# A state-space block with a gated mixture of experts: gated products and mixed adapter values kept in place in PSUM

## The reference

```
x = x + tanh(g_xattn) * ssm(ctx, layernorm(x))        # a scan over 512 positions, 16 states
x = x + tanh(g_ffn)   * moe(layernorm(x))

def _fused_linear(x, W, qa, qb, scale, w):
    out = x @ W.T
    a = jnp.einsum('th,krh->tkr', x, qa)
    b = jnp.einsum('tkr,khr->tkh', a, qb)
    mix = jnp.einsum('tkh,tk->th', b, w)
    return out + scale[None, :] * mix
...
def expert(muW, gW, gqa, gqb, gs, uW, uqa, uqb, us, dW, dqa, dqb, ds, w):
    xe = x + w @ muW.T
    gate = jax.nn.silu(_fused_linear(xe, gW, gqa, gqb, gs, w))
    up = _fused_linear(xe, uW, uqa, uqb, us, w)
    return _fused_linear(gate * up, dW, dqa, dqb, ds, w)
```

## Time and profile before

| | |
|---|---|
| median of 3 runs | 1738.85 us (1738.04 to 1742.68) |
| the profiled execution, its own time | 1740.07 us |
| its span, first to last instruction | 1738.3 us |
| PE busy | 1581.6 us, 91% |
| DVE busy | 1171.5 us, 67% |
| POOL, ACT busy | 719.9 us (41%), 621.4 us (36%) |
| PE on the chain that ended last | 63% of the span |
| DVE on that chain | 19% |

### The profile page before, as it was taken

The page is one execution under the profiler, slowest core; times in us unless marked ns, Lnnn a source line. Parts: engine busy times, 40 slices in busy tenths (PEclk is TensorE's granted clock), DMA queues, the critical chain, the costliest instruction groups (busy, mean ns, idle before and its releaser), DMA issues.

```text
span 1738.3 us, 19493 instructions
## 1 busy us (share of the span) xinstructions
PE 1581.6 (91%) x6856; PEld 1162.7 (67%) x6856; DVE 1171.5 (67%) x1629; ACT 621.4 (36%) x973; POOL 719.9 (41%) x524
## 2 busy tenths in 40 slices
PE   4676778888888899999999999999999999999999
PEld 2243456566666667777777777677767787777776
DVE  5786847588898885578888857588888653333333
ACT  5543334444454433433343334443343311111111
POOL 2465513169888850137677601167777100000000
PEclk7798979989999999999999999999999999999999
DMA  3344625878878766558665554756666357456652
GB/s 132 126 165 169 251 81 184 268 264 286 281 260 284 270 239 237 195 201 276 242 223 199 195 189 167 240 211 233 235 238 234 129 199 239 168 192 219 212 189 82
DMA packets 109888, 365.15 MB, mean 210 GB/s; under 512 B 20000, under 2 KB 45600, under 8 KB 94048
## 3 DMA queue, kind: packets, MB, share of 16 engines
q1 hardware_dynamic: 100320, 330.09, 54.3%
q10 hardware_dynamic: 9472, 33.82, 5.7%
HBM read 293.62 MB, written 70.25 MB: 209 GB/s over the span
## 4 chain that ended last, share of the span: by engine, by line
PE 63%; DVE 19%; ACT 7%; issue 6%; DMA 2%; POOL 2%; SPq 0%; ACTq 0%; DVEq 0%; POOLq 0%
PE b_g L653 14%; PE b_u L653 13%; PE b_u L744 7%; DVE ring L1389 4%; PE b_q L744 4%; PE b_q L699 3%; PE b_g L744 3%; DVE ring L1395 3%; PE b_g L717 3%; PE b_g L684 2%; DVE tt L1363 2%; PE b_g L677 2%; ACT b_a L878 1%; PE b_d L636 1%; DVE z L1363 1%
## 5 line engine op out<-in xcount | busy, mean ns | idle before, releaser
L1286 POOL TENSOR_TENSOR ring<-du,rep 128x512 f32<-128x512 f32 x256 | 335.4, 1315 | 199.1 <-DVE du L1464 115.5
L653 PE MATMUL b_g<-xnb,gm 128*128 128x512 f32 (+1 forms) x1440 | 358.2, 398 | 3.0 <-DVE tt L1363 1.5
L653 PE MATMUL b_u<-xnb,gm 128*128 128x512 f32 (+1 forms) x1440 | 349.4, 391 | 1.4 <-DVE xx L1363 1.4
L1389 DVE TENSOR_TENSOR_SCAN ring<-b_a,ring 128x512 f32<-128x512 f32 x256 | 310.6, 1213 | 55.4 <-ACT b_a L878 42.9
L1295 POOL TENSOR_TENSOR yx<-yx,ring 128x512 f32<-128x512 f32 x192 | 262.3, 1366 | 147.7 <-DVE ring L1395 146.5
L653 PEld LDWEIGHTS b_g<-xnb,gm 128*128 128x128 f32 (+1 forms) x1440 | 253.6, 180 | 92.0 <-issue 27.0
L653 PEld LDWEIGHTS b_u<-xnb,gm 128*128 128x128 f32 (+1 forms) x1440 | 257.0, 179 | 73.1 <-DVE xx L1363 2.2
L1363 DVE SCALAR_TENSOR_TENSOR tt<-tt,b_g 128x512 f32<-128x512 f32 (+1 forms) x120 | 81.9, 683 | 208.7 <-ACT tt L878 208.5
L878 ACT ACTIVATE b_a<-delta,a_neg 128x512 f32<-128x512 f32 x256 | 171.8, 679 | 79.1 <-DVE ring L1389 77.0
L744 PE MATMUL b_u<-dwt,hhl 128*128 128x512 f32 (+1 forms) x720 | 186.4, 395 | 0.4 <-DVE hhl L1366 0.4
L878 ACT ACTIVATE tt<-b_g 128x512 f32<-128x512 f32 (+1 forms) x120 | 71.2, 593 | 288.6 <-PE b_u L684 261.0
(11 more groups left out here) (214 smaller groups left out, 2153.2 us busy)
## 6 DMA issues: line engine op xcount, KB each, us to landing
gm<-scr_gm SPq DMA_DIRECT2D x60, 1024.0 KB, 7.8
dwt<-scr_dw SPq DMA_DIRECT2D x30, 1536.0 KB, 6.8
rep<-bc_d ACTq DMA_DIRECT2D x64, 512.0 KB, 5.0
gm<-scr_gm SPq DMA_DIRECT2D x30, 768.0 KB, 4.4
dqt<-scr_dq SPq DMA_DIRECT2D x24, 896.0 KB, 9.6
scr_gm<-gm SPq DMA_DIRECT2D x20, 1024.0 KB, 7.4
scr_dw<-dwt SPq DMA_DIRECT2D x10, 1536.0 KB, 6.2
qat<-scr_qa SPq DMA_DIRECT2D x24, 512.0 KB, 10.6
```

The source lines that it names most:

```text
L653: i = mm(out_b[0:IW[m], :], w, v, start=(n == 0), stop=(n == 11 and not is_routed(s)))
L1286: v.tensor_tensor(ring[:, T % NRING], du[:, T % 4, :], rep[:, N % NREP, 0], ALU.mult).then_inc(pool_dbu, 1)
L1389: v.tensor_tensor_scan(w, ba[T % 2][:], w, 0.0, ALU.mult, ALU.add).then_inc(dve_scan, 1)
```

## The change

Three values move from SBUF into the PSUM bank from which they were computed. h is written over its gate bank `bg[m]` instead of `tt`; `aw` over `b_q`; `dawf` over `b_g0`. ACT rounds from the bank and DVE subtracts from the bank. No instruction is added, removed or reordered on any engine.

Since a bank now holds the value until its low part is made, waits move. Before a later product may write the bank, PE waits for the low part: for chunk 2's gate product and for the next body's first (`up_waits`), for the first `down` product into `b_g1`, for the first `adapter_a` product into `b_g0`, for the `down` product into `b_q`. And ACT's tanh, which writes `tt`, now waits for h where it waited for the low part.

```diff
             def up_waits(s, m):
                 ready(pe, "gm%d" % m, s)
                 if m == 0:
-                    need(pe, dve_h, IC * s)
+                    need(pe, dve_hl, IC * s)
                     if s > 0 and is_routed(s - 1):
-                        pe.wait_ge(dve_dawf, rho(s - 1) + 1)
+                        pe.wait_ge(dve_daw, rho(s - 1) + 1)
                 elif m == 1:
                     need(pe, dve_dn, LC * (s - 1) + 3)
                 else:
-                    pe.wait_ge(dve_h, IC * s + 1)
+                    pe.wait_ge(dve_hl, IC * s + 1)
...
             def adapter_a(s, m):
-                pe.wait_ge(dve_hl, IC * s + m + 1)
                 if m == 0:
                     ready(pe, "dq", s)
-                    pe.wait_ge(dve_h, IC * s + IC)
+                    pe.wait_ge(dve_hl, IC * s + IC)
...
             def down(s, tc, ms=range(IC)):
...
                         ready(pe, "dw", s)
-                        pe.wait_ge(dve_h, IC * s + 2)
+                        pe.wait_ge(dve_hl, IC * s + 2)
...
-                            pe.wait_ge(dve_aw, rho(s) + 2)
+                            pe.wait_ge(dve_awl, rho(s) + 2)
...
             def tanh(s, m):
-                need(act, dve_hl, IC * s + (0, -1, 1)[m])
+                need(act, dve_h, IC * s + (0, -1, 1)[m])
...
-                rounded(hh[0:w, m], tt[0:w, m % 2, :]).then_inc(act_hh, 1)
+                rounded(hh[0:w, m], bg[m][0:w, :]).then_inc(act_hh, 1)
...
-                stt(t, t, 0.5, bu[m][0:w, :], ALU.mult, ALU.mult).then_inc(dve_h, 1)
+                stt(bg[m][0:w, :], t, 0.5, bu[m][0:w, :], ALU.mult, ALU.mult).then_inc(dve_h, 1)
...
-                lo(hl[0:w, m], t, hh[0:w, m]).then_inc(dve_hl, 1)
+                lo(hl[0:w, m], bg[m][0:w, :], hh[0:w, m]).then_inc(dve_hl, 1)
...
-                tt_(aw[:], b_q[:], wr[:, r % 2], ALU.mult).then_inc(dve_aw, 1)
+                tt_(b_q[:], b_q[:], wr[:, r % 2], ALU.mult).then_inc(dve_aw, 1)
...
-                lo(aw_l, aw[:], aw_h).then_inc(dve_awl, 1)
+                lo(aw_l, b_q[:], aw_h).then_inc(dve_awl, 1)
...
-                tt_(dawf[:], b_g0[:], wr[:, r % 2], ALU.mult).then_inc(dve_dawf, 1)
+                tt_(b_g0[:], b_g0[:], wr[:, r % 2], ALU.mult).then_inc(dve_dawf, 1)
...
-                stt(daw_s[:], rnd[:].bitcast(F32), mlo[:], dawf[:], ALU.mult, ALU.add).then_inc(dve_daw, 1)
+                stt(daw_s[:], rnd[:].bitcast(F32), mlo[:], b_g0[:], ALU.mult, ALU.add).then_inc(dve_daw, 1)
```

More of the change, by code:

```diff
@@ L1059, in aw_hi @@
                 act.wait_ge(pe_gu, IC * s)
-                rounded(aw_h, aw[:]).then_inc(act_aw, 1)
+                rounded(aw_h, b_q[:]).then_inc(act_aw, 1)
             def daw_round(s):
                 act.wait_ge(dve_dawf, rho(s) + 1)
-                rounded(rnd[:], dawf[:]).then_inc(act_daw, 1)
+                rounded(rnd[:], b_g0[:]).then_inc(act_daw, 1)
             def shared_0(b, pre_):
```

## The result

The changed kernel takes 1759.95 us (median of 4 runs, 1759.58 to 1760.25), the kernel before 1738.44 beside it; the ratio is 1.0118, 95% interval [1.0101, 1.0136]. That is 21.5 us more, where 14.7 were forecast. The profiled execution took 1759.88 us with a span of 1758.1, so its span is 19.8 longer than that of before. Where they went, by the start of each body's first up product (into `b_u0`) in the two traces: 1.6 us ahead of batch 0's first body, 3.5 in batch 0, 6.0 in batch 1, 7.8 in batch 2, nothing in the first nine bodies of batch 3, 0.9 in the last.

A forecast was written before the change was run, and what follows sets the result against it. PE was taken as the bound from batch 1 on, DVE and PE alternating in batch 0. Batches 1 and 2 (+8.1), last body (+0.7), batch 0 (+2.5) and clock dips (+3.4) give +14.7, 1753.5 us; range 1741 to 1766.

The forecast's parts named there:

- PE as the bound from batch 1 on: Routed bodies from batch 1 on: PE is busy nearly throughout (248.57 of 253 us in batch 2), so its delays add time.
- The six products and the low part: At adapter_a, six products lose 1.36 us of cover; low parts shorten from 1.40 to 0.69: +8.1 us over batches 1 and 2.
- A bank as operand: DVE's low part and h write using PSUM: low part 0.69 us everywhere, h's write bounded by 0.03 either way, taken as 0.
- The clock: Longer PE gaps at adapter_a in experts 0 and 4 bring two new clock dips, +3.4 us, up to +8.5.
- Batch 0: All eight bodies wait at adapter_a, less DVE's gain on low parts and daw_s: +2.5 us, bounds -4 to +9.6.
- rival B: Faster: DVE's chain sets the pace in batches 0 to 2, so its savings shorten bodies; -8.5, 1730 us, chance 0.08.
- The other moved waits are covered: Chunk 2's gate product, the b_q down product and the next body's first product lose nothing, though narrowly.
- The sum: Whole kernel: 8.1 + 0.7 + 2.5 + 3.4 = +14.7 us, forecast 1753.5 us.

The follow-up runs named there:

- experiment 1: Kernel before with only adapter_a's wait moved to chunk 2's low part, every value in SBUF: 1772.39 us, ratio 1.0191.
- experiment 7: Kernel before with h in its gate banks for chunks 0 and 1 only, chunk 2 in SBUF: 1739.11 us; with six down products also moved ahead, 1729.09.
- Experiment 5: Kernel before with h in place in the up product's banks instead of the gate product's, aw and dawf in SBUF: 1728.41 us, ratio 0.9935.
- experiment 4: Changed kernel with adapter_a writing b_u0 and dawf in SBUF: 1734.52 us, ratio 0.9978; with aw also back in SBUF and its old wait: 1729.42, 0.9953.
- experiment 6: Six fourth-chunk down products moved ahead of adapter_a: in the changed kernel 1726.71 us, ratio 0.9935; in the kernel before 1730.78, ratio 0.9958.

## Why the prediction was right, and where its sizes were off

**PE as the bound from batch 1 on** was right: in batches 1 to 3 a body whose nine adapter products had no wait for the low part kept its length to 0.03 us, and a body in which they had one became longer by it, dips aside. PE's idle time in front of these products went from 31.3 us to 47.2 in all, 15.9 more where some 15 were forecast.

**The six products and the low part** were right in sign and nearly in size: 0.67 to 0.69 in experts 2 and 6 where 0.65 stood, 1.37 for 1.3, 0.09 for 0.1. Without dips the batches cost 4.4 and 4.6 us instead of 4.05. Of what is missing in expert 4 and in the last body, 0.2 is one thing: PE starts 0.14 to 0.15 us behind the low part's end, where the row of before had 0.05, and nine products take 2.32 behind a wait and 2.22 without. I had counted the latter in expert 0 only. Expert 4 of batch 2 lost 1.09, 0.4 more than the 0.7 forecast; the other 0.2 is there because chunk 2's low part begins 28.94 us behind the body's first gate product where it was 28.66. The last body: 0.15 + 0.10 on top of 0.7 is 0.95; it was 0.93.

**A bank as operand** cost nothing, as I took from the rows: all 120 low parts lie between 678 and 694 ns. The Trainium skill, "VectorE: DVE Perf Modes", section on the TRN2 errata, has 62 cycles more of fixed cost for a PSUM source; by that rule they would be 65 ns longer, and the trace does not show it: 690 ns from a bank, 690 from SBUF without POOL.

**The clock** was right in that new dips come with longer waits, and at about their price; the rule by which they were placed, that the longest gaps bring them, failed. 3.4 us were forecast for two new dips among experts 0 and 4, and three came: one at expert 0 in batch 2, and two at expert 3, where none was forecast, for 1.65 + 1.6 + 1.6 = 4.9. Expert 3 in batch 2, and the stretches around it, with the granted clock last but two:

```profile
1253.78 0.68 DVE L1365 TENSOR_TENSOR hhl<-b_g,hhl 96x512 fp32r<-96x512 f32 x1
...
1254.60 2.98 PE L716 MATMUL b_g<-hhl,dqt 128*128 128x512 f32 x9 [2.25 <-DVE hhl L1365]
...
1257.39 1.48 PE L743 MATMUL b_g<-dwt,hhl 96*128 96x512 f32 x3
```

```profile
1250.00:1254.00 4.00, 2.35 (x11) 1.62 (x9) 3.97 (x7) 1.28 (x2) 2.42 (x3) 1.00 0.62 209
1254.00:1258.00 4.00, 3.40 (x11) 2.75 (x12) 3.74 (x6) 1.18 (x2) 3.48 (x3) 0.75 0.00 0
```

The wait made the body some 0.65 longer and the dip behind it 1.6 more: three `down` products take 1.48 us instead of 0.85. Expert 4 of the same batch had the longer gap, and none:

```profile
1295.44 2.33 PE L716 MATMUL b_g<-hhl,dqt 128*128 128x512 f32 x9 [3.54 <-DVE hhl L1365]
```

```profile
1290.00:1294.00 4.00, 1.90 (x9) 1.24 (x7) 2.72 (x4) 1.15 (x2) 3.33 (x3) 1.00 0.15 58
1294.00:1298.00 4.00, 2.56 (x11) 2.15 (x12) 3.39 (x5) 1.75 (x4) 1.68 (x3) 1.00 0.00 0
```

**Batch 0** is where the prediction's working failed. Its bounds held, but that the forecast of +2.5 came near the measured 3.5 is luck. I set PE's loss (9.6) against DVE's gain (7.1) and put the clock at nothing. For the seven bodies of experts 1 to 7, here are PE's waits (us in total, times, longest) and the stretch's busy times, before and then after:

```profile
PE b_g L717 <- DVE hhl L1366: 11.7, 6, 3.6
PE b_g L717 <- DVE tt L1363: 8.2, 6, 2.2
PE b_g L744 <- DVE hhl L1366: 5.9, 6, 1.7
PE b_q L699 <- DVE qat L1366: 4.6, 5, 2.5
```

```profile
371.00:668.00 297.00, 264.33 (x1152) 193.73 (x1151) 254.71 (x315) 130.38 (x196) 225.11 (x154) 0.97 0.75 267
```

```profile
PE b_g L716 <- DVE hhl L1365: 24.3, 7, 6.0
PE b_g L743 <- issue: 5.7, 6, 2.1
PE b_q L699 <- DVE qat L1365: 2.5, 1, 2.5
```

```profile
373.00:673.00 300.00, 267.18 (x1152) 199.24 (x1151) 245.04 (x313) 128.93 (x195) 213.83 (x153) 0.94 0.74 264
```

With two lines of 1.1 each that are left out here, PE waited 32.6 us before, and 32.5 after. The losses and gains in waiting cancel out, and the 2.9 us by which these bodies grew are PE's own: 1152 products take 267.2 us instead of 264.3, at a granted clock of 0.94 instead of 0.97. The waits are the same in sum but in fewer and longer pieces, 14 instead of 27, the longest 6.0 instead of 3.6. It is tempting to take this for the cause of the lower clock, but the other traces don't bear it out. The kernel of experiment 1 has 15 pieces in these bodies, the longest 7.2, 38.7 us in sum, and its PE took 264.6 us, as before, at a clock that is 0.94 too; that of experiment 7 has 23 pieces, none above 3.2, 28.0 in sum, and took 267.6. What sets the clock in batch 0 stays open. Experiment 5 shows these bodies where `adapter_a`'s wait does not move: they take 288.6 us (297.6 before, 300.6 with the change), with 28.1 us of waits, at a clock of 0.98:

```profile
371.00:659.00 288.00, 259.69 (x1152) 191.14 (x1151) 248.10 (x315) 129.16 (x196) 222.94 (x154) 0.98 0.77 277
```

So 9 us were to be had in these bodies and 3 were lost. Of the 9, 4.5 are waits and 4.6 PE's own time at the higher clock. "Faster" (rival B) has its mechanism right in part: DVE is busy 6.6 us less in these bodies there, the values of the adapter still in SBUF, and the waits shrink by 4.5, where B counted 9.2 with those values. In the changed kernel the moved wait took all of it.

**"The other moved waits are covered"** holds nearly for the changed kernel in batches 1 and 2: from 1115 to 1402 us PE waits 9.7 us in 5 times for the adapter, and besides that once for 0.5 us at the first `down` product of expert 0, where it had 0.2. In the second body of batch 0, a half of the shared expert, it does not hold. Chunk 2's gate product waits 2.9 us for chunk 0's low part, where it had waited 1.5 for that chunk's h (before, then after, from 240 to 371 us):

```profile
PE b_g L653 <- DVE tt L1363: 1.5, 1, 1.5
```

```profile
PE b_g L653 <- DVE hhl L1365: 2.9, 1, 2.9
```

And the cover of the wait for aw's low part was the first loss itself. Fifteen products against 2.9 us counted the six that had been delayed; whoever repairs the first wait and not the second keeps some 4 us of loss, as experiment 4 shows (ratios 0.9978 and 0.9953).

**The sum.** 19.8 us of span against 14.7 are 5.1 more: 0.9 in the waits of batches 1 and 2, 0.2 in the last body, 1.5 in their dips, 1.0 in batch 0, and 1.6 ahead of the first body, in a setup that the change doesn't touch (the parts are rounded). Measured the same way, that start is at 246.2 us before and lies between 245.4 and 249.2 in the other kernels, with nothing changed ahead of it, and batch 0 of the kernel with only aw's wait moved came out 3 us shorter than that of before. One trace of batch 0 is thus good to some 3 us at best, and its 3.5 are hardly more than that, though the kernel with h alone has nearly the same: 3.7 in batch 0, and in the seven bodies 14 waits of 32.8 us and 268.0 us of PE time. The traces of batches 1 and 2 are good to 0.1, dips aside.

## What to carry to other kernels

Before a value is kept in a bank, ask who takes that bank next and what cover that work gives: here one bank of the two gives a gain (11 us in all, with DVE's low parts at half the time under POOL), and the other turns it into a loss of 21. Price moved waits one at a time as well as together, since a loss may be what hides the next one. And read TensorE's own time beside its waits: at the same 28.0 us of waits the same products took 260.7 us in one kernel and 267.6 in another, at granted clocks of 0.98 and 0.95.

## What the hardware showed that I had not expected

- A longer gap on PE does not bring a dip by itself: 2.25 us of idling were followed by a half-speed stretch and 3.54 us were not, 40 us later in the same batch. In the kernel of experiment 5, expert 0 of batch 2 had a dip (1.5 us) that the kernels of experiments 4, 6 and 7 don't have. In the kernel with aw's wait alone moved, expert 4 of batch 2 has the gap of before (2.49 us, 2.47 before) and a stretch at half clock behind it that before has not. What decides was not tried.
- At full clock a PE that starts behind a semaphore takes 2.32 us for nine products and one that runs on takes 2.22, so a wait costs 0.1 us more than the gap that the trace shows. The gap itself has 0.14 to 0.15 from the end of the instruction that was waited for to the start.
- ACT's rounding of h (128x512, means of 60 from 240 to 1402 us) takes 592 ns from a bank and 627 from SBUF, DVE's write to a bank 695 and to SBUF 687. Keeping h in a bank makes the way from the product to its high part 27 ns shorter, not longer.
